# The third pass of key and value products in the wide attentions, split over two halves of the array and the unused rows of another pass

## The chip, the cores and the metric

One core of a Trainium2 chip runs the whole program in one launch. The metric is device time in microseconds (us) of that execution; the time of the kernel before is the median of three runs. TensorE multiplies on a 128x128 array, ScalarE, VectorE and GpSimd (POOL in the profile) do elementwise work, and SyncE (SP) issues DMAs. Results of TensorE go to PSUM, whose eight banks hold 512 fp32 columns each.

## The reference

A stack of four pairs of layers, each a cross-attention and a feed-forward part, all added to a residual x of 128 batches x 64 rows x 128 channels. Three of the four cross-attentions are wide (layers 0, 1 and 3 of the reference): 8, 8 and 16 heads of 64 channels, over a context of 64 rows x 96 channels per batch.

```python
x = x + jnp.tanh(g_xattn[0]) * _L0_xattn_ref(_layernorm(x, axis=-1), ctx_768, mask_BxS2_bk0, ...)
...
# in a wide attention
q = (x @ W_q).reshape(b, n, HEADS, DIM_HEAD)
k = (context @ W_k).reshape(b, j, HEADS, DIM_HEAD)
v = (context @ W_v).reshape(b, j, HEADS, DIM_HEAD)
sim = jnp.einsum('bihd,bjhd->bhij', q, k) * scale
attn = jax.nn.softmax(jnp.where(mask, sim, max_neg), axis=-1)
out = jnp.einsum('bhij,bjhd->bihd', attn, v).reshape(b, n, INNER)
return out @ W_o + b_o
```

Layer 3 has one more key and value per head (null_kv), a layernorm with a gain before, and another behind. All is fp32. The change touches only how k and v are computed from the context.

## The kernel before

**Stages.** `program` runs eight stages one after another. Stages 0, 2 and 6 call `wide_attention` for layers 0, 1 and 3; `null` is true for layer 3. In the trace they lie at about 0 to 325 us, 965 to 1300 us and 2325 to 2985 us.

**Groups, units, tiles.** x has 64 tiles of 128 rows (two batches of 64), in 16 groups of TG = 4. A unit (`Unit`) is one group with eight heads: layers 0 and 1 have 16 units, layer 3 has 32 (two passes over a group, u = 0 and u = 1). Every engine walks the same loop: iterations `it`, two units `u`, four tiles `t`, one `step` each, so 64, 64 and 128 steps, 256 in all. The first and the last iteration are written out, the ones between are a loop on the chip.

**Three products for one.** An fp32 product is made of three fp32r products: each operand is split into a high part and the rest, high x high, high x low and low x high are summed in PSUM (`product3`, whose lines L384, L385 and L386 name the three). `ch`/`cl` are the parts of the transposed context of a unit (96 channels on partitions 0 to 95, 512 columns), `kh`/`kl`, `qh`/`ql`, `wvh`/`wvl` those of the weights. The values need a layout of their own, `vh`/`vl`, which POOL makes from `ch`/`cl` (`spread`, L576 and L577). In layer 3 partition 96 of `vh` and `wvh` carries the null value.

**One step of TensorE**, in the order of its queue: transpose the probabilities of tile n (L778), project the output of tile n-1 (L722), `attend` (L712, 64x64 tiles of the array), `scores` of tile n+2 (L700, 64x64 tiles), in some steps `turn` (L669: transpose the normed rows of a later group into hT), `value_job` of tile n+1 (six products of 256 columns), `key_job` (three products of 512 columns with 96 rows) and `query_job` (three products of 512 columns with 128 rows) for a later unit. `turn` comes where t = 1: in every unit of layers 0 and 1 but the last two, and in layer 3 with u = 0 only. `target_of` says which unit the keys are for: a unit's first two key blocks are made at t = 2 and 3 two units ahead, the others at t = 0 and 1 one unit ahead. The last iteration has keys in its first two steps only.

**Banks and waits.** Keys go to bank 1, queries to bank 0, values to bank 4, but to bank 0 for t = 1; the transposes (L778 and L669) use bank 4 as well. ScalarE empties them in this order in each step: transposed probabilities (L912), queries of the step before (L833), attention output (L919, L921), then hT (L842, where there is a turn), values (L837), the high part of hT (L846), keys (L828), exponentials of tile n+2 (L850). In layer 3 the high part of hT comes last, after the queries. TensorE's query at t = 1 waits for `v_done` (the value copy, same bank), its attend for `pt_out` (L912), its scores at t = 2 for the last query copy (L833).

**Context.** SP loads the raw context of a unit (L528), waiting for `low`; POOL splits it at t = 0 two units ahead (L561 high, L563 low, after its wait `k_done`). In layer 0 SP issues the loads of everything later (`boot.sync_third`, L193 and L195) between the first iteration's waits and the loop:

```python
            n = units // 2
            body(0, False)
            if boot:
                boot.sync_third(sp)
            if n > 3:
                with sp.Fori(1, n - 2) as it:
                    body(it, False)
```

Of the kernel before, what the change touches and what calls it, by code (L numbers as in the profile page):

```python
# [5 lines left out]
FP = mybir.dt.float32  # L6
# [422 lines left out]
def wide_attention(c, d, layer, boot=None):  # L429
# [34 lines left out]
    hh, hl = [r([GT]) for _ in range(nhq)], [r([GT]) for _ in range(nhq)]  # L464
    (kh, kl), (qh, ql), (wvh, wvl) = ((r([WN]), r([WN])) for _ in range(3))
    if masked:
        mask = c.mask
        nm = [w([TG, SW]), w([TG, SW])]
    if null:
# [19 lines left out]
    o_ready, ot_out, acc_ready, added, nm_ready = (sem(n) for n in ("o", "ot_out", "acc", "added", "nm"))  # L489
    acc_out, edges = sem("acc_out"), sem("edges")  # L490
    fin_bn, fin_mv, fin_eps, fin_rstd, fin_y, fin_yg = (
        sem(n) for n in ("fbn", "fmv", "feps", "frstd", "fy", "fyg"))
# [31 lines left out]
    with nc.Block() as block:  # L524
        @block.sync
        def _(sp):
# [8 lines left out]
            if boot:  # L535
                boot.sync_second(sp)

            def body(it, last):
# [126 lines left out]
        def _(te):  # L665
# [16 lines left out]
            def value_job(un, t, out):  # L682

                if t == 0:
                    te.wait_ge(spread_ready, un.k * 2 + 2)
                for e in range(2):
                    at = (un.p * 2 + e) * NJ * DH
                    lhs = [v[un.u][0:VR, t, e:e + 2, :].rearrange("c b k -> c (b k)") for v in (vh, vl)]
                    last = product3(c, out[:, e * NJ * DH:(e + 1) * NJ * DH], lhs, [v[0:VR, at:at + NJ * DH] for v in (wvh, wvl)])
                last.then_inc(v_full, 1)  # L690
# [77 lines left out]
            def step(it, u, t, last):  # L768
# [21 lines left out]
                if t < 2 or not end:  # L790
# [6 lines left out]
                    scores(n + 2, *two_on(un, t))  # L797
                if turns(u, t, last):
                    turn(un.g + 1 if null else un.k + 2)
                if not (end and t == TG - 1):  # L800
                    if t == 1 and had_target(it, u, t, last):
                        te.wait_ge(q_done, n + 6)
# [22 lines left out]
        def _(act):  # L825
# [48 lines left out]
            if null:  # L874
                for i in range(2):
                    last_row = slice(DC, DC + 1)
                    ones = bc(c.w["ones"][last_row, :], 1, TG * 3 * S // P)
                    A.activation(vh[i][last_row, :, :, :].rearrange("c t b k -> c (t b k)").rearrange("c (n k) -> c n k", k=P), ones, ACT.Copy,
                                 scale=-1.0)
                    A.activation(vl[i][last_row, :, :, :].rearrange("c t b k -> c (t b k)").rearrange("c (n k) -> c n k", k=P), ones, ACT.Copy,  # L880
                                 scale=0.0)
# [24 lines left out]
            def body(it, last):  # L906
                for u in range(2):
                    for t in range(TG):
# [1689 lines left out]
def program(nc, d, layers=range(8)):  # L2598

    ctx = ExitStack()  # L2600
    with ctx:
# [15 lines left out]
        for layer in layers:  # L2617

            parts = {0: 8 * GT + 12 * P * 2 + 24 * D, 2: 8 * GT + 12 * P * 2 + 24 * D, 5: 4 * GT + 4 * W2N, 6: 6 * GT + 12 * P * 2 + 48 * D}
            c.open_work({0: 15 * 1024, 2: 15 * 1024, 6: 14 * 1024, 5: 12 * 1024}.get(layer, 26 * 1024) - TG * P, parts.get(layer, 0))  # L2620
            if layer in (0, 2, 6):
# [98 lines left out]
```

## Time and profile before

| | |
|---|---|
| median of 3 runs | 3075.03 us (3073.38 to 3079.5) |
| profiled execution | 3082.58 us, span of its instructions 3080.6 us |
| granted TensorE clock, mean | 0.977 |
| TensorE busy | 2901.3 us (94%) |
| VectorE busy | 2225.0 us (72%) |
| ScalarE busy | 1579.8 us (51%) |
| POOL busy | 1182.4 us (38%) |
| DMA | 211.98 MB |

The profile is one execution. Matmuls are pipelined: the duration that a row gives runs to the end of the last column, so rows overlap and starts tell more than durations. A product's start is that of its slot in the array; where its weights could not be loaded ahead, the load is inside its slot, and shows as a later start of the product behind it. A time in a row of the timeline is the start from the beginning of the span.

### The profile page before, as it was taken

The numbers are of one execution on the slowest core, as the hardware profiler recorded it, in microseconds if no ns is written. First come the engines' busy times: TensorE is split into PE (matmuls) and PEld (weight loads), VectorE is DVE, ScalarE is ACT, GpSimd is POOL, SyncE is SP. The second block draws the span as 40 slices with busy tenths as digits, with TensorE's granted clock in tenths as the row PEclk, the third lists the DMA queues.
The fourth block names the chain that finished last, engine by engine and source line by source line (L and its number), as shares of the span: only waits on it lengthen the run. The fifth ranks groups of instructions, "written<-read, shape, count | busy, mean of one in ns | idle before, by whom it ended". The sixth has DMA issues, their size and how long they took to land. (4 is left out here: it accounts for less than half of the span.)

```text
span 3080.6 us, 89544 instructions
## 1 busy us (share of the span) xinstructions
PE 2901.3 (94%) x34642; PEld 2264.9 (74%) x34642; DVE 2225.0 (72%) x5778; ACT 1579.8 (51%) x2906; POOL 1182.4 (38%) x1274
## 2 busy tenths in 40 slices
PE   7999799999998999859997999999998999999978
PEld 6888545555546888746666888888886888888864
DVE  6777666666655666568887777788766788878766
ACT  6777311211113777537774333333336777777756
POOL 6677200000003777564450000000004677777753
PEclk9999899999999999979998999999998999999989
DMA  5000166666661000011111333323330000000001
GB/s 157 20 10 8 62 187 178 182 181 179 184 169 35 12 10 10 2 52 27 25 26 57 111 105 104 105 97 96 106 112 16 12 10 9 9 10 10 10 1 55
DMA packets 110872, 211.98 MB, mean 69 GB/s; under 512 B 18738, under 2 KB 30450, under 8 KB 110195
## 3 DMA queue, kind: packets, MB, share of 16 engines
q1 hardware_dynamic: 110194, 208.98, 22.8%
q8 instruction: 89, 1.46, 0.2%
q10 hardware_dynamic: 512, 0.92, 0.1%
q14 instruction: 77, 0.62, 0.1%
HBM read 198.29 MB, written 5.77 MB: 66 GB/s over the span
## 5 line engine op out<-in xcount | busy, mean ns | idle before, releaser
L384 PE MATMUL ps<-parts 128*128 128x512 f32 (+3 forms) x1568 | 623.3, 398 | 34.1 <-DVE parts L1002 18.2
L385 PE MATMUL ps<-parts 128*128 128x512 f32 (+3 forms) x1568 | 565.1, 360 | 0.0
L386 PE MATMUL ps<-parts 128*128 128x512 f32 (+3 forms) x1568 | 563.7, 359 | 0.0
L318 POOL TENSOR_TENSOR rstd<-mv,eps 128x4 f32<-128x4 f32 x106 | 21.2, 200 | 998.4 <-DVE mv L301 998.2
L1941 ACT ACTIVATE work<-ps 128x512 f32<-128x512 f32 x272 | 162.5, 598 | 441.9 <-PE ps L386 441.7
L384 PEld LDWEIGHTS ps<-parts 128*128 128x128 f32 (+2 forms) x1568 | 299.4, 191 | 106.3 <-ACT work L837 26.4
L582 POOL TENSOR_TENSOR work<-work 128x512 f32<-128x512 f32 x256 | 266.9, 1043 | 278.1 <-DVE work L972 278.1
L386 PEld LDWEIGHTS ps<-parts 128*128 128x128 f32 (+2 forms) x1568 | 298.8, 191 | 46.0
L385 PEld LDWEIGHTS ps<-parts 128*128 128x128 f32 (+2 forms) x1568 | 301.2, 192 | 20.6
L1906 PEld LDWEIGHTS ps<-early,work 128*128 128x128 f32 x2176 | 281.5, 191 | 18.8 <-DVE pause L1995 0.3
L1906 PE MATMUL ps<-early,work 128*128 128x128 f32 x2176 | 288.0, 275 | 0.1
L1991 DVE TENSOR_TENSOR work<-work,ps 128x512 f32<-128x512 f32 x272 | 185.7, 683 | 122.0 <-PE ps L1906 107.5
L970 DVE TENSOR_REDUCE work<-work 128x8 f32<-128x512 f32 (+1 forms) x256 | 174.0, 680 | 127.1 <-ACT work L850 125.5
L2276 PE MATMUL ps<-work,early 128*128 128x512 f32 x512 | 248.1, 607 | 1.3 <-DVE work L2518 1.3
L837 ACT ACTIVATE work<-ps 128x512 f32<-128x512 f32 x256 | 153.1, 598 | 149.1 <-PE ps L386 146.1
L958 DVE SCALAR_TENSOR_TENSOR ps<-ps,work 128x520 f32<-128x520 f32 (+1 forms) x192 | 135.2, 704 | 130.6 <-PE ps L700 130.0
L962 DVE TENSOR_REDUCE work<-ps 128x8 f32<-128x512 f32 (+1 forms) x256 | 178.0, 695 | 53.8 <-PE ps L700 47.1
L712 PE MATMUL ps<-work 64*64 64x64 f32 x8192 | 179.3, 224 | 11.6 <-ACT work L912 9.5
L2518 DVE TENSOR_TENSOR work<-work 128x1024 f32<-128x1024 f32 x128 | 154.7, 1219 | 47.5 <-DMA work<-gate_rows 45.5
L2001 DVE TENSOR_TENSOR work<-work 128x512 f32<-128x512 f32 x256 | 177.2, 692 | 12.7 <-DVE work L1991 0.2
L964 DVE TENSOR_TENSOR work<-ps,work 128x512 f32<-128x512 f32 (+1 forms) x256 | 178.0, 695 | 8.8
L712 PEld LDWEIGHTS ps<-work 64*64 64x64 f32 x8192 | 145.4, 134 | 44.5 <-issue 16.9
(296 smaller groups left out, 6072.6 us busy)
## 6 DMA issues: line engine op xcount, KB each, us to landing
work<-gate_rows SPq DMA_DIRECT2D x128, 512.0 KB, 5.7
work<-expert_rows SPq DMA_DIRECT2D x512, 128.0 KB, 2.9
work<-gate_rows SPq DMA_DIRECT2D x128, 256.0 KB, 7.0
work<-in_ctxT SPq DMA_DIRECT2D x72, 192.0 KB, 2.4
out<-x SPq DMA_DIRECT2D x16, 256.0 KB, 2.3
work<-work SPq DMA_DIRECT2D x224, 16.0 KB
work<-work SPq DMA_DIRECT2D x16, 128.0 KB, 2.3
early<-in_l0f_w SPq DMA_DIRECT2D x1, 1536.0 KB
```

What stands on the lines that cost most here:

```text
L384: T.matmul(out, lh, rh, start=True, stop=False)
L385: T.matmul(out, lh, rl, start=False, stop=False)
L386: return T.matmul(out, ll, rh, start=False, stop=True)
L582: G.tensor_tensor(pn[t % 2], pr[t % 2][:, :, 0:S], bc(rec[t % 2], 2, S), ALU.mult).then_inc(p_ready, 1)
L712: last = T.matmul(ps_o[e * DH:e * DH + DH, b, j, :], vp[t % 2][rows, e, j, :], ptT[rows, j, b * S:b * S + S], start=True, stop=True)
L962: V.tensor_reduce(mx[t % 2], ps_s, AX.X, ALU.max).then_inc(max_ready, 1)
L964: V.tensor_tensor(sc[t % 2].rearrange("p (j s) k -> p s j k", s=2), ps_s.rearrange("p (s j) k -> p s j k", s=2), bc(tops, 3, SW), ALU.subt ...
L970: V.tensor_reduce(den[t % 2], pr[t % 2], AX.X, ALU.add).then_inc(sum_ready, 1)
L1906: last = T.matmul(acc[u][:, t * D:(t + 1) * D], aT[b][:, t * P:(t + 1) * P], c.w["l2f_d"][:, j, :], start=(j == 0 and t == 0), stop=(j == ...
L1991: out = V.tensor_tensor(aT[b], sg[b], ps_u[b], ALU.mult)
L2001: V.tensor_tensor(aT[b], aT[b], wb[j % WR], ALU.mult).then_inc(a_ready, 1)
L2276: T.matmul(ps_q[u], c.w["l0f_w"][:, at:at + P], hw[p % NHW][:, e, :], start=(p == 0 and e == 0), stop=(p == NP - 1 and e == 1))
```

## The change

The low x high product of keys and values is cut in two. Of the 96 rows of the high x low pass, 32 are put beside the 96 rows of the low x high pass (partitions 96 to 127, which were idle), and the other 64 become products of their own on half of the array: for the keys on partitions 64 to 127 (`key_third`), for the values on partitions 0 to 63 (`value_third`), issued one behind the other, with different banks. Both come right after the scores; then the rest of the values, the turn, the rest of the keys, the query. ScalarE copies the values before hT. Which of the rows lie where:

- keys, half product: weights `kl` 64 to 127, data `ch` 64 to 127; rows 96 to 127 hold copies of rows 0 to 31;
- keys, 128-row product: `kh` and `cl`, whose rows 96 to 127 hold copies of rows 32 to 63 of `kl` and `ch`;
- values, half product: `vh` and `wvl`, rows 0 to 63; 128-row product: `vl` and `wvb`, whose rows 96 to 127 hold rows 64 to 95 of the context's high part and of `wvl`. `wvb` is `wvh` itself, and a buffer of its own in layer 3.

The copies are made by DMAs from SBUF to SBUF that SP issues. Layer 3's prologue loses two activations that set the null row of `vl` to zero (L880), and the null row's low part moves into row 97 of `wvh`.

```diff
+            def rows_for_keys(un):
+                sp.wait_ge(high, un.k + 1)
+                sp.dma_start(plain(ch[un.u][DC:P, :]), plain(ch[un.u][0:P - DC, :])).then_inc(key_rows[un.u], 16)
+                sp.dma_start(plain(cl[un.u][DC:P, :]), plain(ch[un.u][P - DC:S, :])).then_inc(key_rows[un.u], 16)
+            def rows_for_values(un):
+                src = plain(ch[un.u][S:DC, :]).rearrange("c (t b k) -> c t b k", b=2, k=S)
+                sp.dma_start(plain(vl[un.u][DC:P, :, 0:2, :]), src).then_inc(value_rows[un.u], 16)
+                sp.dma_start(plain(vl[un.u][DC:P, :, 2, :]), src[:, :, 0, :]).then_inc(value_rows[un.u], 16)
+            rows_for_keys(first)
+            rows_for_values(first)
+            sp.wait_ge(w_low, passes)
+            sp.dma_start(plain(kl[DC:P, :]), plain(kl[0:P - DC, :])).then_inc(weight_rows, 16)
+            sp.dma_start(plain(kh[DC:P, :]), plain(kl[P - DC:S, :])).then_inc(weight_rows, 16)
+            rows_for_keys(second)
+            rows_for_values(second)
+            sp.wait_ge(w_low, 3 * passes)
+            sp.dma_start(plain(wvb[DC:P, :]), plain(wvl[S:DC, :])).then_inc(weight_rows, 16)
...
             def body(it, last):
                 for u in range(2):
                     un = Unit(it, u, passes)
+                    rows_for_keys(un.next().next())
                     if not (u == 1 and isinstance(it, int) and it == units // 2 - 2):
                         sp.wait_ge(low, un.k + 3)
                         load(cs, cs_in, un.next().next().next())
+                    sp.wait_ge(v_full, un.k * 4 + 4)
+                    rows_for_values(un.next().next())
...
                 if raw is cs:
                     pool.wait_ge(cs_in, (un.k - 1) * 16)
+                    pool.wait_ge(value_rows[un.u], un.it * 32)
...
+            def key_third(un, j, bank):
+                T.matmul(jobs[bank], kl[S:P, at:at + P], ch[un.u][S:P, :], start=True, stop=False)
+            def key_rest(un, j, bank):
+                T.matmul(jobs[bank], kh[0:DC, at:at + P], ch[un.u][0:DC, :], start=False, stop=False)
+                T.matmul(jobs[bank], kh[:, at:at + P], cl[un.u], start=False, stop=True).then_inc(k_full, 1)
+            def value_third(un, t, out):
+                for e in range(2):
+                    T.matmul(out[:, e * NJ * DH:(e + 1) * NJ * DH], vh[un.u][0:S, t, e:e + 2, :].rearrange("c b k -> c (b k)"),
+                             wvl[0:S, at:at + NJ * DH], start=e == 0, stop=False, skip_group_check=True)
+            def value_rest(un, t, out):
+                for e in range(2):
+                    T.matmul(dst, high_rows[0:VA, :], wvh[0:VA, cols], start=False, stop=False, skip_group_check=True)
+                    last = T.matmul(dst, low_rows, wvb[:, cols], start=False, stop=e == 1, skip_group_check=True)
...
-                if turns(u, t, last):
-                    turn(un.g + 1 if null else un.k + 2)
-                if not (end and t == TG - 1):
-                    value_job(*one_on(un, t), value_bank(t))
-                if has_target(u, t, last):
-                    key_job(target, j, 1)
+                if opening:
+                    te.wait_ge(weight_rows, WEIGHT_ROWS)
+                if keys:
+                    if t == 2 or opening:
+                        te.wait_ge(key_rows[target.u], target.it * 32 + 32)
+                    key_third(target, j, 1)
+                if values:
+                    if t == TG - 1 or opening:
+                        te.wait_ge(value_rows[value_unit.u], value_unit.it * 32 + 32)
+                    value_third(value_unit, value_tile, value_bank(t))
+                    value_rest(value_unit, value_tile, value_bank(t))
+                if turns(u, t, last):
+                    turn(un.g + 1 if null else un.k + 2)
+                if keys:
+                    key_rest(target, j, 1)
...
+                        if not (end and t == TG - 1):
+                            take_values(n + 1, t + 1, value_bank(t))
                         if turns(u, t, last):
                             take_hT(un.g + 1 if null else un.k + 2)
-                        if not (end and t == TG - 1):
-                            take_values(n + 1, t + 1, value_bank(t))
```

## Rows read from the trace of the kernel before

**Rows 1.** Windows: each engine's busy us, clock, DMA; layer 3's loop.

```profile
2370.00:2970.00 600.00, 594.57 (x10775) 519.09 (x10774) 475.00 (x1169) 452.32 (x800) 419.48 (x428) 1.00 0.03 10
```

**Rows 2.** Timeline of TensorE, a plain step of layer 1: start, duration, line.

```profile
1120.30 0.38 PE L384 MATMUL ps<-parts 96*128 96x256 f32 x1
1120.53 0.28 PE L385 MATMUL ps<-parts 96*128 96x256 f32 x1
...
1121.12 0.40 PE L384 MATMUL ps<-parts 96*128 96x512 f32 x1
...
1121.81 0.40 PE L384 MATMUL ps<-parts 128*128 128x512 f32 x1
```

**Rows 3.** Timeline of TensorE where the form of the tile changes, other stages.

```profile
514.61 1.16 PE L2296 MATMUL ps<-work 64*128 64x128 f32 x8
515.70 1.12 PE L2276 MATMUL ps<-work,early 128*128 128x512 f32 x2
...
3031.73 1.14 PE L1692 MATMUL ps<-work,l3f_v 32*128 32x512 f32 x8
3032.80 1.12 PE L1684 MATMUL ps<-work,l3f_u 128*128 128x512 f32 x2
```

**Rows 4.** Timeline of ScalarE, a step with a turn in layer 1.

```profile
1071.53 0.60 ACT L842 ACTIVATE work<-ps 128x512 f32<-128x512 f32 x1 [0.50 <-PE ps L669]
1072.16 0.60 ACT L837 ACTIVATE work<-ps 128x512 f32<-128x512 f32 x1
1072.65 0.62 ACT L846 ACTIVATE parts<-work 128x512 fp32r<-128x512 f32 x1
...
1073.66 0.63 ACT L850 ACTIVATE work<-work 128x512 f32<-128x512 f32 x1
1074.25 0.60 ACT L912 ACTIVATE work<-ps 128x512 f32<-128x512 f32 x1
1074.74 0.59 ACT L833 ACTIVATE work<-ps 128x512 f32<-128x512 f32 x1
```

**Rows 5.** Timeline of TensorE in the same step and the next.

```profile
1070.76 0.66 PE L669 MATMUL ps<-ident,hn 128*128 128x128 f32 x4
...
1072.81 0.50 PE L384 MATMUL ps<-parts 128*128 128x512 f32 x1
...
1073.61 0.60 PE L778 MATMUL ps<-ident,work 128*128 128x128 f32 x4
1074.05 1.06 PE L722 MATMUL ps<-early,work 128*128 128x128 f32 x8
...
1075.68 0.69 PE L700 MATMUL ps<-work 64*64 64x64 f32 x32
```

**Rows 6.** Timelines of ScalarE and TensorE, layer 3, u = 1, t = 1.

```profile
2539.95 0.60 ACT L837 ACTIVATE work<-ps 128x512 f32<-128x512 f32 x1 [0.66 <-PE ps L386]
2540.61 0.50 PE L384 MATMUL ps<-parts 128*128 128x512 f32 x1
```

**Rows 7.** Timeline of SP in layer 0: first load of `sync_third`, next context load.

```profile
57.65 0.43 SPq L193 DMA_DIRECT2D l_wo<-in_l_wo  x1
...
88.99 0.35 SPq L528 DMA_DIRECT2D work<-in_ctxT  x1
```

**Rows 8.** Timeline of ScalarE in layer 0: copy of unit 1's last values.

```profile
65.41 0.60 ACT L837 ACTIVATE work<-ps 128x512 f32<-128x512 f32 x1 [0.75 <-PE ps L386]
```

**Rows 9.** Timeline of TensorE in layer 0, unit 2: t = 0 and t = 2.

```profile
77.24 0.58 PE L384 MATMUL ps<-parts 96*128 96x256 f32 x1
...
81.25 1.06 PE L778 MATMUL ps<-ident,work 128*128 128x128 f32 x4
...
90.33 0.39 PE L384 MATMUL ps<-parts 96*128 96x256 f32 x1
```

**Rows 10.** DMA issues of the page: count, KB each, us from issue to landing.

```profile
work<-in_ctxT SPq DMA_DIRECT2D x72, 192.0 KB, 2.4
```

**Rows 11.** One line's instructions (L880): duration ns min/median/max, first and last start.

```profile
L880 ACT ACTIVATE parts<-ones x2: 822/822/823, 2329.8 to 2331.7; 1x768 fp32r<-1x768 f32 x2
```

More of the change, by code:

```diff
@@ L465, in wide_attention @@
     (kh, kl), (qh, ql), (wvh, wvl) = ((r([WN]), r([WN])) for _ in range(3))
+    wvb = r([WN]) if null else wvh
+    plain = lambda ap: ap.bitcast(FP)
     if masked:
@@ L490, in wide_attention @@
     acc_out, edges = sem("acc_out"), sem("edges")
+    weight_rows = sem("weight_rows")
+    key_rows, value_rows = [sem(f"key_rows{u}") for u in range(2)], [sem(f"value_rows{u}") for u in range(2)]
+    WEIGHT_ROWS = 16 * (5 if null else 3)
     fin_bn, fin_mv, fin_eps, fin_rstd, fin_y, fin_yg = (
@@ L536, in _ @@
                 boot.sync_second(sp)
+            def rows_for_keys(un):
[15 more added lines that the diff above has]
+            sp.dma_start(plain(wvb[DC:P, :]), plain(wvl[S:DC, :])).then_inc(weight_rows, 16)
+            if null:
+                sp.dma_start(plain(wvb[0:DC, :]), plain(wvh[0:DC, :])).then_inc(weight_rows, 16)
+                sp.dma_start(plain(wvh[DC + 1:DC + 2, :]), plain(wvl[DC:DC + 1, :])).then_inc(weight_rows, 16)
             def body(it, last):
@@ L682, in value_job @@
             def value_job(un, t, out):
-                if t == 0:
-                    te.wait_ge(spread_ready, un.k * 2 + 2)
+                te.wait_ge(spread_ready, un.k * 2 + 2)
                 for e in range(2):
                     at = (un.p * 2 + e) * NJ * DH
-                    lhs = [v[un.u][0:VR, t, e:e + 2, :].rearrange("c b k -> c (b k)") for v in (vh, vl)]
-                    last = product3(c, out[:, e * NJ * DH:(e + 1) * NJ * DH], lhs, [v[0:VR, at:at + NJ * DH] for v in (wvh, wvl)])
+                    cols = slice(at, at + NJ * DH)
+                    dst = out[:, e * NJ * DH:(e + 1) * NJ * DH]
+                    high_rows, low_rows = (v[un.u][:, t, e:e + 2, :].rearrange("c b k -> c (b k)") for v in (vh, vl))
+                    T.matmul(dst, high_rows[0:VR, :], wvh[0:VR, cols], start=True, stop=False)
+                    T.matmul(dst, high_rows[0:VR, :], wvl[0:VR, cols], start=False, stop=False)
+                    last = T.matmul(dst, low_rows[0:DC, :], wvh[0:DC, cols], start=False, stop=True)
@@ new lines, in value_job @@
+                last.then_inc(v_full, 1)
+            def key_third(un, j, bank):
+                at = un.p * NJ * P + j * P
+                T.matmul(jobs[bank], kl[S:P, at:at + P], ch[un.u][S:P, :], start=True, stop=False)
+            def key_rest(un, j, bank):
+                at = un.p * NJ * P + j * P
+                T.matmul(jobs[bank], kh[0:DC, at:at + P], ch[un.u][0:DC, :], start=False, stop=False)
+                T.matmul(jobs[bank], kh[:, at:at + P], cl[un.u], start=False, stop=True).then_inc(k_full, 1)
@@ L797, in step @@
                     scores(n + 2, *two_on(un, t))
-                if turns(u, t, last):
-                    turn(un.g + 1 if null else un.k + 2)
-                if not (end and t == TG - 1):
-                    if t == 1 and had_target(it, u, t, last):
-                        te.wait_ge(q_done, n + 6)
-                    value_job(*one_on(un, t), value_bank(t))
-                if has_target(u, t, last):
+                values, keys = not (end and t == TG - 1), has_target(u, t, last)
+                opening = isinstance(it, int) and it == 0 and u == 0 and t == 0
+                if opening:
+                    te.wait_ge(weight_rows, WEIGHT_ROWS)
+                if keys:
                     target, j = target_of(un, t)
@@ L811, in step @@
                         te.wait_ge(low, target.k + 1)
-                    key_job(target, j, 1)
+                    if t == 2 or opening:
+                        te.wait_ge(key_rows[target.u], target.it * 32 + 32)
+                    key_third(target, j, 1)
+                if values:
+                    if t == 1 and had_target(it, u, t, last):
+                        te.wait_ge(q_done, n + 6)
+                    value_unit, value_tile = one_on(un, t)
+                    if t == TG - 1:
+                        te.wait_ge(spread_ready, value_unit.k * 2 + 2)
+                    if t == TG - 1 or opening:
[6 more added lines that the diff above has]
+                    key_rest(target, j, 1)
                     if t == 1:
@@ L2617, in program @@
         for layer in layers:
-            parts = {0: 8 * GT + 12 * P * 2 + 24 * D, 2: 8 * GT + 12 * P * 2 + 24 * D, 5: 4 * GT + 4 * W2N, 6: 6 * GT + 12 * P * 2 + 48 * D}
-            c.open_work({0: 15 * 1024, 2: 15 * 1024, 6: 14 * 1024, 5: 12 * 1024}.get(layer, 26 * 1024) - TG * P, parts.get(layer, 0))
+            parts = {0: 8 * GT + 12 * P * 2 + 24 * D, 2: 8 * GT + 12 * P * 2 + 24 * D, 5: 4 * GT + 4 * W2N, 6: 6 * GT + 12 * P * 2 + 56 * D}
+            c.open_work({0: 15 * 1024, 2: 15 * 1024, 6: 14 * 1024 - 256, 5: 12 * 1024}.get(layer, 26 * 1024) - TG * P, parts.get(layer, 0))
             if layer in (0, 2, 6):
```

14 lines of the change are left out of this document (9 added, 5 removed).

## The prediction

> **What bounds the kernel now.** I read first the busy time of each engine over the steady part of the last wide attention, which is the longest. TensorE is busy 594.6 of 600 us there, at the full 2.4 GHz clock (granted 1.00), ScalarE 452 [rows 1]. So a step (one 128-row tile, eight heads) lasts as long as TensorE's own order of work, and what TensorE's queue gains or loses per step is gained or lost 256 times, unless a wait stands behind it. Second, TensorE's timeline of one plain step [rows 2]: from the first value product to the first query product it is 1121.81 - 1120.30 = 1.51 us. The reader should see two spacings in it. A 256-column product follows the one before after 0.12 us ((1121.12 - 1120.53)/5), a 512-column one after 0.23 us ((1121.81 - 1121.12)/3); but the first value product, which comes right after the 64x64 scores, holds its successor up by 0.23 instead of 0.12. Third, other stages, for what happens where the form of the tile changes [rows 3]. Fourth, ScalarE's and TensorE's timelines around the turn of hT [rows 4, 5] and in the second tile of a group without one [rows 6], since ScalarE's order is edited. Last, SP's queue in layer 0 [rows 7 to 9], since new waits go into it.
>
> **What the packed third is worth.** Removed from TensorE's stream: one 512-column key product (0.23) that now runs beside two 256-column value products (2 x 0.12). Do halves run side by side? In the low-rank stage four row groups with two passes each, all 128 columns wide into four banks, take 3032.80 - 3031.73 = 1.07 us for eight 512-column passes [rows 3], when even eight fp32r products at 0.23 would need 1.84 one after another. So yes.
>
> Added: one more change of tile form. Before, a step goes 128-wide to 64x64 (attend, scores) to 128-wide; now 64x64 to 64x128 to 128x128. The price: eight 64-row passes between two 128-row stages take 515.70 - 514.61 = 1.09 us [rows 3]. Such a 128-column pass is 0.11 in the unbroken stream of transposes ((1074.05 - 1073.61)/4 [rows 5]), 0.89 for eight: 0.20 more, and 0.11 of it is the weight load that is not hidden behind a product (as 0.23 against 0.12 in [rows 2]), 0.09 a drain. The Trainium skill's page "TensorEngine Tiling (Array Packing)", Key Properties, says that changing the tiling mode drains TensorE. The trace agrees, with these 0.09 us for each change; the page has no price and says nothing of the weight load behind it.
>
> New stretch, from the same start T: load 0.11, first value third 0.12, second 0.12 (the key third ends in the same time, 0.11 + 0.23), drain 0.09 gives the form 128x128 at T+0.43; load 0.11, four value products 0.47, two key products 0.46: the query begins at T+1.475. Gain 0.035 us per plain step instead of the 0.23 that the packing seems to offer. Bounds for the change 64x64 to 64x128, which no row shows: nothing (gain 0.235), or as much as every other change (0.035). I take the latter, because a change of rows alone and of both dimensions costs the same in [rows 3].
>
> A step with values but no keys (5 at each layer's end) only pays: 2 x 0.12 + 0.20 - 2 x 0.12 = 0.20.
>
> **ScalarE.** The value copy starts when the last value product ends. That product now starts at T+0.89 instead of T+0.70 (0.23 + 4 x 0.12), so v_done is 0.19 later although the query is due earlier. The product is 0.28 long [rows 2] and the copy starts some 0.04 after its end (an estimate by the 0.06 between copy and query in [rows 6]): T+1.21. In the second tile (t = 1) the values lie in bank 0, which the query needs.
> Without a turn (layer 3, second unit): the query begins 0.06 after the end of the copy already, 2540.61 against 2539.95 + 0.60 [rows 6], and this moves by +0.19. Cost +0.19 for 15 steps.
> With a turn (T' = 1070.76, start of the transposes): before, the query starts at T'+2.05, held by the copy; then the next step's transposes at T'+2.85, its scores at T'+4.92 [rows 5]. Now the turn stands between values and keys, and the query is free: transposes at T'+0.89+0.12+0.44+0.46+0.70 = T'+2.61. But ScalarE's chain starts at T'+1.21 instead of T'+0.77 (1071.53 [rows 4]): value copy 1.21, hT 1.70 (spacing 0.49 as 1072.16 to 1072.65), its high part 2.33 (it needs the finished hT, 0.60, and a little), key copy and exponentials in the spacing 1.01 of 1072.65 to 1073.66: 3.34, then the copy of the transposed probabilities 0.49 to 0.59 later (the latter in 1073.66 to 1074.25, where it waited for TensorE), I take 0.53, 3.87, the query copy 0.49 on, 4.36, done 4.95. Scores begin 0.35 after that end now (1075.68 against 1074.74 + 0.59 [rows 4, 5]): T'+5.30. So this step loses 0.38 where it should win 0.035. It comes 14 times in each of layers 0 and 1. In layer 3 the high part is made after the queries, outside this chain: between 0 and 0.38, I take 0.10, 15 times.
>
> Sums: layers 0 and 1, 28 units x (0.38 - 3 x 0.035) = +7.7. Layer 3, 15 pairs of units x (0.10 + 0.19 - 5 x 0.035, the first step of a group gaining nothing since it waits for the copy of acc) = +1.7. Layer ends 15 x 0.20 = +3.0.
>
> **SP's queue in layer 0.** The new rows are filled by DMAs that SP issues, two for keys and two for values a unit: 32 rows of 2 KB each, landing some 2.4 us after issue like the context load [rows 10]. In steady state the key rows are issued when POOL has the high part in t = 0 and are read in t = 2, two steps on; value rows have five steps. Hidden. Not so once: after the first pair of units SP issues the loads of all later layers. That took from 57.65 to 88.99, 31.3 us [rows 7]. Before, it began when POOL had split unit 3. Now SP first waits for all values of unit 1 (v_full), which ScalarE takes at 65.41 [rows 8], then issues two more: start 66.4, end 97.7, and only behind it come the key rows of unit 4, landing about 97.7 + 0.9 + 2.4 = 101. TensorE wants them with the key third at 90.33 [rows 9], shifted by about 0.4: a pause of 10.3 us. Queued behind that wait is everything on TensorE, so also ScalarE, VectorE and POOL. After an idle stretch it restarts at 1.2 GHz: 81.25 - 77.24 = 4.01 us from value to transposes [rows 9] against 1.51 + 0.70 in [rows 2], 1.8 more; with the following step 2.5. Sum +12.8. Bounds: 0 if the rows land in time, 16 if the later loads also run slower beside them.
> In layer 0's prologue the weight rows and first rows queue behind the loads of x and are due with the first step; I take nothing, bounds 0 and one landing, 2.4 [rows 10]. In layer 3's prologue two activations of 0.82 us go, ahead of the first key copies [rows 11]: between 0 and -1.64, I take -0.95, since hT's copy behind them also waits for transposes.
>
> Sum: 7.7 + 1.7 + 3.0 + 12.8 - 0.95 = +24.3 us. The profiled execution took 3082.6 (span 3080.6); against it 3106.9, against the median of the runs, 3075.0, it is 3099.3.
>
> **Rivals.**
> (a) The change 64x64 to 64x128 is free, because rows stay at 64. Then 238 steps with both thirds and 15 without keys win 0.20 each: 3099 - 51 = 3048, faster. For it: no row shows this pair. Against: every pair that is shown pays. It decides from about half the price: with under 0.10 saved per step the kernel is still not faster. 14%.
> (b) No pause in layer 0 (SP is through earlier, or rows overtake the loads): 3099 - 13 = 3086, still slower. For it: the last nine loads are limited by issue, not by data. 15%.
> (c) ScalarE keeps up in the turn steps, whose wait for the value copy (0.26) then vanishes: 28 x (0.38 + 0.26) = 18 less, 3081. With (b) 3068. For it: ScalarE has 25% free; against: the chain above. 10%, a third of it with (b).
> (d) The halves do not run side by side: 238 x 0.23 more, 3154. For it: no fp32r product with 64 rows is shown. The Trainium skill's page "TensorE: Matmul & The Clock Gate", Measured speedup vs the span model, gives 3.07 for four row tiles instead of 4; by that the pair would take 0.31 instead of 0.24, an estimate of 238 x 0.07 = 16 us more. 6%.
> My forecast (all prices as worked out) has 55%; its own range is 3088 to 3112.
>
> **How the numbers follow.** A measurement tells 0.2% (6 us) from no change. Faster: (a) and (b with c), 18%, and a little for (c) turning out better: 20%. Same: what is left of (c) and of mixed cases, 8%. Slower 72%. For 8 in 10 the range leaves out most of (a) and (d) and takes in (b), (c): 3070 to 3115.
>
> **What the profile after would show.** TensorE's plain step: L700, then a 512-column product and two 256-column ones within 0.01 and 0.23 us, the first 128x128 product 0.43 after the block's start; step length 4.68 instead of 4.72. In t = 1 with a turn the next scores some 0.38 later, with ScalarE without a gap from value copy to query copy. One pause of TensorE near 91 us, released by a DMA. Wrong if plain steps are 4.5 us (a), 4.9 (d), if no pause is there (b), or if turn steps shrink (c).

## The result, and the profile after

The changed kernel takes 3111.53 us (median of 4 runs, 3109.38 to 3113.28) against 3074.35 before (4 runs, 3073.38 to 3079.5): 1.0113 times as long, 95% interval 1.0101 to 1.0126. The forecast was 3099.3, slower. Its profiled execution took 3113.28 us with a span of 3111.3, 30.7 more than the profiled execution before; the medians differ by 37.2. Against its own median the profile before lies 8.2 us high and that after 1.8, so 6.5 us of the difference cannot be placed in the two traces.

The length of a step below is the distance between the first transposes of successive steps (L778 before, L845 after). Over the 64, 64 and 128 steps of the three wide attentions the distance from the first to the last grew from 318.2 to 341.0 us (layer 0), 306.5 to 311.7 (layer 1) and 628.5 to 631.8 (layer 3): 31.3 in all, as much as the two spans differ by. Within the kinds of step it looks like this (medians, us; where a row has values for odd and even units, units are counted from 0, so even is u = 0):

| step | before | after |
|---|---|---|
| layer 1, t = 0 / t = 3 | 4.716 / 4.718 | 4.713 / 4.714 |
| layer 1, t = 1 (turn) | 5.367 | 5.197 |
| layer 1, t = 2 (odd / even units) | 4.773 / 4.900 | 5.223 / 5.462 |
| layer 3, u = 0: t = 1 (turn), t = 2 | 5.759, 5.027 | 5.559, 5.343 |
| layer 3, u = 1: t = 1 | 4.991 | 5.187 |
| layer 1, the five last steps with values and no keys | 4.27, 4.30, 4.30, 3.36, 4.41 | 4.46, 4.49, 4.50, 3.56, 4.53 |

First the plain step. TensorE's timeline of the kernel after, layer 1 (start, duration, line), to be read against [rows 2]:

```profile
1105.81 0.50 PE L732 MATMUL ps<-parts 64*128 64x512 f32 x1
1105.81 0.50 PE L744 MATMUL ps<-parts 64*128 64x256 f32 x2
1106.24 0.38 PE L755 MATMUL ps<-parts 96*128 96x256 f32 x1
1106.46 0.28 PE L756 MATMUL ps<-parts 128*128 128x256 f32 x1
1106.59 0.28 PE L755 MATMUL ps<-parts 96*128 96x256 f32 x1
1106.71 0.28 PE L756 MATMUL ps<-parts 128*128 128x256 f32 x1
1106.82 0.40 PE L737 MATMUL ps<-parts 96*128 96x512 f32 x1
1107.07 0.40 PE L738 MATMUL ps<-parts 128*128 128x512 f32 x1
1107.30 0.40 PE L384 MATMUL ps<-parts 128*128 128x512 f32 x1
```

The key half product (L732) and the first value half product (L744) start together, and the first product on the whole array (L755, 96 of its rows, form 128x128) follows 0.43 us later. Then see the four starts from 1106.24 on: the first successor comes after 0.22, the others after 0.12 or 0.13. That 0.22 is the second change of form, paid as at the first product before. Three whole products have become three halves that share their time, and two changes of form are there where one was: from the block's start to the query it is 1.49 us, against 1.51.

Second, the turn. ScalarE's timeline of the kernel after, a step with a turn in layer 1, against [rows 4]; the block of half products starts at T' = 1115.24:

```profile
1116.46 0.60 ACT L918 ACTIVATE work<-ps 128x512 f32<-128x512 f32 x1 [0.95 <-PE ps L756]
1116.95 0.59 ACT L923 ACTIVATE work<-ps 128x512 f32<-128x512 f32 x1
1117.58 0.63 ACT L927 ACTIVATE parts<-work 128x512 fp32r<-128x512 f32 x1
1118.11 0.58 ACT L909 ACTIVATE work<-ps 128x512 f32<-128x512 f32 x1
1118.59 0.62 ACT L931 ACTIVATE work<-work 128x512 f32<-128x512 f32 x1
1119.11 0.59 ACT L991 ACTIVATE work<-ps 128x512 f32<-128x512 f32 x1
1119.59 0.60 ACT L914 ACTIVATE work<-ps 128x512 f32<-128x512 f32 x1
```

Seven activations without a gap. Counted from T', values, hT, its high part, exponentials, transposed probabilities and queries start at 1.22, 1.71, 2.34, 3.35, 3.87 and 4.35; the forecast had 1.21, 1.70, 2.33, 3.34, 3.87 and 4.36. TensorE in the same step, against [rows 5]:

```profile
1115.24 0.50 PE L732 MATMUL ps<-parts 64*128 64x512 f32 x1
...
1117.17 0.44 PE L384 MATMUL ps<-parts 128*128 128x512 f32 x1
...
1117.92 0.60 PE L845 MATMUL ps<-ident,work 128*128 128x128 f32 x4
...
1119.84 0.69 PE L779 MATMUL ps<-work 64*64 64x64 f32 x32 [0.43 <-ACT work L991]
1120.33 0.68 PE L767 MATMUL ps<-work 64*64 64x64 f32 x32
```

TensorE is done with its turn step earlier, and then its attend (L779) stands 0.43 us for the copy of the transposed probabilities (L991), the sixth link of ScalarE's chain. So t = 1 shrinks and t = 2 grows by more. This is an odd unit, where the scores (L767) follow the attend by 0.49. In the even units of the same layer the attend stands 0.46 for the same copy and the scores follow it by 0.69; they begin 0.35 after the end of the query copy (L914), as they do in the even units of the kernel before. Counted from T', scores begin at 5.09 in odd units and 5.32 in even ones, against 4.79 and 4.92 before. In layer 3 with u = 1, where there is no turn, the query waits for the value copy, both 0.19 later, against [rows 6]:

```profile
2567.22 0.60 ACT L918 ACTIVATE work<-ps 128x512 f32<-128x512 f32 x1 [0.86 <-PE ps L756]
...
2567.86 0.50 PE L384 MATMUL ps<-parts 128*128 128x512 f32 x1 [0.21 <-ACT work L918]
```

Third, layer 0. TensorE's timeline and then SP's of the kernel after, against [rows 7 to 9]:

```profile
86.94 0.69 PE L767 MATMUL ps<-work 64*64 64x64 f32 x32
104.73 0.79 PE L732 MATMUL ps<-parts 64*128 64x512 f32 x1 [17.10 <-DMA parts<-parts]
...
108.61 1.05 PE L845 MATMUL ps<-ident,work 128*128 128x128 f32 x4
```

```profile
68.34 0.59 SPq L193 DMA_DIRECT2D l_wo<-in_l_wo  x1
...
98.65 0.43 SPq L195 DMA_DIRECT2D tri<-in_tri  x1
99.31 0.56 SPq L546 DMA_DIRECT2D parts<-parts  x1
99.92 0.58 SPq L547 DMA_DIRECT2D parts<-parts  x1
```

One pause of 17.1 us, ended by a DMA from SBUF to SBUF. SP spends 68.34 to 99.31 on the loads of later layers, and only behind them it issues the key rows (L546, L547) of unit 4. Behind the pause TensorE runs slowly, at a granted clock of 0.50 from 104 to 108 us: from block to transposes it is 3.88 us, against 2.17 us in the next step (112.03 to 114.20). The waits of TensorE over the whole program (total us, count, longest) put the two that grew side by side (for the first, the kernel before has 9.5 us in 14 waits), and the windows of layer 3, against [rows 1], show that there the array stays the bound:

```profile
PE ps L779 <- ACT work L991: 24.1, 52, 1.5
PE ps L732 <- DMA parts<-parts: 18.4, 2, 17.1
```

```profile
2400.00:3000.00 600.00, 587.46 (x10684) 501.01 (x10682) 471.05 (x1163) 436.05 (x794) 416.35 (x425) 1.00 0.08 21
```

### The profile page after: what moved, and what is told of

It is laid out like the page before. It is cut to its first block and busy times, and to the rows that moved or that the text cites. A ratio compares the mean times of both kernels' runs of the same rounds, so it can differ in the third digit from the quotient of the medians.

```text
span 3111.3 us, 90063 instructions
## 1 busy us (share of the span) xinstructions
PE 2897.9 (93%) x34642; PEld 2240.0 (72%) x34642; DVE 2224.8 (72%) x5778; ACT 1552.7 (50%) x2904; POOL 1181.2 (38%) x1274
## 5 line engine op out<-in xcount | busy, mean ns | idle before, releaser
L384 PE MATMUL ps<-parts 128*128 128x512 f32 (+1 forms) x818 | 356.7, 436 | 37.6 <-DVE parts L1081 17.8
L386 PE MATMUL ps<-parts 128*128 128x512 f32 (+1 forms) x818 | 325.7, 398 | 0.0
L385 PE MATMUL ps<-parts 128*128 128x512 f32 (+1 forms) x818 | 325.6, 398 | 0.0
L1985 PEld LDWEIGHTS ps<-early,work 128*128 128x128 f32 x2176 | 281.8, 192 | 18.9 <-DVE pause L2074 0.3
L384 PEld LDWEIGHTS ps<-parts 128*128 128x128 f32 (+1 forms) x818 | 157.3, 192 | 86.9 <-ACT work L918 21.6
L779 PE MATMUL ps<-work 64*64 64x64 f32 x8192 | 178.6, 224 | 24.6 <-ACT work L991 24.1
L779 PEld LDWEIGHTS ps<-work 64*64 64x64 f32 x8192 | 145.4, 135 | 58.4 <-issue 34.6
L386 PEld LDWEIGHTS ps<-parts 128*128 128x128 f32 (+1 forms) x818 | 156.0, 191 | 37.4
L610 POOL TENSOR_TENSOR parts<-parts,zero 96x512 fp32r<-96x512 f32 x128 | 166.5, 1300 | 27.6 <-ACT parts L948 27.6
```

Source lines behind the costliest of these rows:

```text
L384: T.matmul(out, lh, rh, start=True, stop=False)
L385: T.matmul(out, lh, rl, start=False, stop=False)
L386: return T.matmul(out, ll, rh, start=False, stop=True)
L779: last = T.matmul(ps_o[e * DH:e * DH + DH, b, j, :], vp[t % 2][rows, e, j, :], ptT[rows, j, b * S:b * S + S], start=True, stop=True)
L1985: last = T.matmul(acc[u][:, t * D:(t + 1) * D], aT[b][:, t * P:(t + 1) * P], c.w["l2f_d"][:, j, :], start=(j == 0 and t == 0), stop=(j == ...
```

## The experiments

All ratios are against the kernel before, run on the same chip (medians 3076.5 to 3078.6 there).

**One: the later loads in parts** (`e1_loads_in_parts`). `sync_third` is cut into four parts, one in each of the units 1 to 4, so that the copies queue behind seven or so loads instead of all.

```diff
                         load(cs, cs_in, un.next().next().next())
+                    if boot and isinstance(it, int) and it * 2 + u in (1, 2, 3, 4):
+                        boot.sync_part(sp, it * 2 + u - 1)
                     sp.wait_ge(v_full, un.k * 4 + 4)
```

> The changed kernel, but in layer 0 SP issues the loads of the later layers in four parts, one in each of units 1 to 4, behind that unit's key rows and ahead of its wait for the values. My theory (the pause of 17.1 us near 87 us is key rows queued behind 31 us of loads): pause and the slow-clock restart behind it go, 19 to 20 us less, about 3091. Rival 1, the copies from SBUF to SBUF are themselves late while anything loads: a pause of several us stays, 5 us less at most. Rival 2, the time is lost elsewhere and the pause was hidden: no change, 3111.

3093.04 us (3089.99 to 3094.71), ratio 1.0043 [1.0026, 1.0060]. Layer 0 is 19.7 us shorter than after the change, 18.9 of it in the step that held the pause; layers 1 and 3 do not move. TensorE of this kernel at the same place:

```profile
87.17 0.69 PE L771 MATMUL ps<-work 64*64 64x64 f32 x32
87.80 0.50 PE L736 MATMUL ps<-parts 64*128 64x512 f32 x1
```

The half product (L736 here) follows the scores at once. The pause is the place of the copies in SP's queue and nothing else.

**Two: hT's high part a step later** (`e2_high_part_later`). ScalarE makes it after the query copy of the turn step, POOL's split moves behind `spread`.

```diff
+                        if turns(u, t - 1, last) and not null:
+                            rows_high(un.k + 2, u)
                         act.wait_ge(o_ready, n + 1)
...
-                        if turns(u, t, last) and not null:
-                            rows_high(un.k + 2, u)
```

> The changed kernel, but in layers 0 and 1 ScalarE makes the high part of hT one step later, behind the query copy of t = 2, and POOL spreads the values' low part before it splits hT. My theory (ScalarE's chain from value copy to query copy holds up attend and scores of t = 2): step t = 2 goes from 5.22 to about 4.77 us, 28 times, 12 to 13 us less, about 3099. Rival, another wait holds t = 2 (POOL's split or the keys): t = 2 stays above 5.1 us and the time moves by less than 3 us, or gets worse because hq_low comes late.

3096.12 us, ratio 1.0059 [1.0042, 1.0076]. In layer 1 step t = 2 goes from 5.223 and 5.462 (odd and even units) to 4.711 and 4.896; over the 14 units that is 7 to 8 us for each of layers 0 and 1. ScalarE's timeline of this kernel:

```profile
1104.37 0.64 ACT L931 ACTIVATE work<-work 128x512 f32<-128x512 f32 x1
1105.02 0.60 ACT L991 ACTIVATE work<-ps 128x512 f32<-128x512 f32 x1
1105.51 0.59 ACT L914 ACTIVATE work<-ps 128x512 f32<-128x512 f32 x1
1105.99 0.63 ACT L927 ACTIVATE parts<-work 128x512 fp32r<-128x512 f32 x1
```

The block of this step starts at 1101.70, so the copy of the probabilities (L991) begins at T' + 3.32 instead of 3.87, and the high part (L927) fills the place where ScalarE otherwise waits. The stall was the order of ScalarE's chain, not its load.

**Three: whole products in the new order** (`e3_whole_thirds`). Everything of the change stays, copies and waits too, but the third pass goes over its 96 rows in one piece, and the 128-row products over 96.

```diff
-                T.matmul(jobs[bank], kl[S:P, at:at + P], ch[un.u][S:P, :], start=True, stop=False)
+                T.matmul(jobs[bank], kl[0:DC, at:at + P], ch[un.u][0:DC, :], start=True, stop=False)
...
-                    last = T.matmul(dst, low_rows, wvb[:, cols], start=False, stop=e == 1, skip_group_check=True)
+                    last = T.matmul(dst, low_rows[0:DC, :], wvb[0:DC, cols], start=False, stop=e == 1, skip_group_check=True)
```

> The changed kernel in its new order and with all its copies, but the third pass is one whole product of 96 rows (97 for null values) for the keys and for each half of the values, so there is one change of tile form less and nothing beside it. My theory (the half products win 0.235 us per step, the extra drain and the weight load take 0.20 back and the products with 128 rows 0.03): plain step 4.716 us, and the layers' last steps 0.2 shorter each, in all 3108 (3104 to 3113). Rival, the drain is not the price and the new order or the copies cost the time: plain step 4.65 or less would be seen, 3095 or less. Rival 2, the halves do win something net: 3120 or more.

3115.8 us (3113.11 to 3116.55), ratio 1.0121 [1.0104, 1.0138], above the range that I had given and not clearly apart from the changed kernel's 1.0113. The plain step is 4.7355, against 4.716 before and 4.713 after. So the half products win 0.022 us net per plain step, but the new order with whole products loses 0.02 against the old one. The timelines show where: the 256-column products, which now stand behind a 512-column one, follow one another after 0.120 us instead of 0.116 to 0.119 (means of layer 1, t = 0), while the 512-column ones keep their distances. Why is not shown.

**Four: both half products on the same half** (`e4_same_half`). The key half product uses rows 0 to 63 instead of 64 to 127, so its sum has other rows in it.

```diff
-                T.matmul(jobs[bank], kl[S:P, at:at + P], ch[un.u][S:P, :], start=True, stop=False)
+                T.matmul(jobs[bank], kl[0:S, at:at + P], ch[un.u][0:S, :], start=True, stop=False)
```

> The changed kernel, but the keys' half product takes rows 0 to 63 instead of 64 to 127, the same half of the array as the values' (so other rows are summed; the sizes are the same). My theory (the halves do run side by side): the key third and the two value thirds then follow one another, the first 128-row product comes 0.66 instead of 0.43 us after the block's start, plain step 4.95, and about 56 to 60 us more, near 3169. Rival (they never ran side by side, or the array shares one stream of moving data): no change, 3111.

3164.75 us, ratio 1.0279 [1.0259, 1.0300]; the plain step 4.911. TensorE's timeline of this kernel:

```profile
1122.28 0.49 PE L732 MATMUL ps<-parts 64*128 64x512 f32 x1
1122.62 0.39 PE L744 MATMUL ps<-parts 64*128 64x256 f32 x2
1122.94 0.39 PE L755 MATMUL ps<-parts 96*128 96x256 f32 x1
```

On one half they take turns, 0.66 us to the first whole-array product instead of 0.43. So on two halves they run at the same time in full; that is worth 0.23 us in the block and 0.20 in the plain step.

**Five: one more change of form** (`e8_one_more_change`). The order is rest of the values, half products, rest of the keys, so that the step has one more pair of 128-row and 64-row stages.

```diff
-                    value_third(value_unit, value_tile, value_bank(t))
                     value_rest(value_unit, value_tile, value_bank(t))
+                if keys:
+                    key_third(target, j, 1)
+                if values:
+                    value_third(value_unit, value_tile, value_bank(t))
```

> The changed kernel with the same products, but the half products stand between the rest of the values and the rest of the keys: the form of the tile goes 64x64, 128x128, 64x128, 128x128, one change more in each step. My theory (a change costs a drain of 0.09 us and a weight load of 0.11): plain step 4.91 us, 0.20 x 241 = 48 us more than the changed kernel and a few more where the value copy is late, ratio near 1.028. Rival, the extra change is cheap and something else eats the gain: plain step 4.75 or less.

3144.86 us, ratio 1.0218 [1.0197, 1.0238]; the plain step is 4.89, 0.18 more than after the change. TensorE's timeline of this kernel:

```profile
1112.44 0.28 PE L757 MATMUL ps<-parts 128*128 128x256 f32 x1
1112.65 0.50 PE L732 MATMUL ps<-parts 64*128 64x512 f32 x1
1112.66 0.50 PE L744 MATMUL ps<-parts 64*128 64x256 f32 x2
1113.08 0.50 PE L737 MATMUL ps<-parts 96*128 96x512 f32 x1
1113.41 0.40 PE L738 MATMUL ps<-parts 128*128 128x512 f32 x1
```

The half products start 0.21 behind a 256-column product instead of 0.12, and the product after the one at 1113.08 comes 0.33 later instead of 0.23. A drain of 0.09 and an uncovered weight load of 0.10 for the additional change, as forecast from other stages. The total grew by 33 us and not by 48. Turn steps grew by only 0.08 to 0.09 and the u = 1, t = 1 step of layer 3 not at all: there the wait for ScalarE covered it. And layer 0's first step, 8.75 us after the change, is 6.19 here, a difference that does not come from this edit (see what the traces differ in, below).

**Six: without the copied rows** (`e9_copied_rows_out`). The rows 96 to 127 are left out of the 128-row products, so the sum lacks 32 rows.

```diff
-                T.matmul(jobs[bank], kh[:, at:at + P], cl[un.u], start=False, stop=True).then_inc(k_full, 1)
+                T.matmul(jobs[bank], kh[0:DC, at:at + P], cl[un.u][0:DC, :], start=False, stop=True).then_inc(k_full, 1)
```

> The changed kernel, but the second product of each rest takes 96 rows instead of 128 (the 32 copied rows of high times low are left out of the sum); everything else, the copies too, stays. The plain step won 0.003 us instead of the 0.035 that I worked out, because the products after the block follow one another 0.003 to 0.012 later than before. Theory A, the switch between 96 and 128 rows costs it: spacings of 0.232 again, plain step 4.68 us, 6 to 8 us less than the changed kernel. Theory B, it is the moment at which these products run, beside what the other engines do, and not their rows: plain step stays 4.71, no change in all.

3111.55 us, ratio 1.0112 [1.0091, 1.0133]. In layer 1 the plain step is 4.688, so 0.025 shorter, which is what theory A asks; the total is that of the changed kernel, and two runs cannot tell 6 us from nothing. The traces show less than 6: layers 1 and 3 are 1.1 us shorter each, since in layer 3 the plain steps won 0.01 to 0.04 and both steps with t = 1 lost 0.02. TensorE's timeline of this kernel:

```profile
1105.13 0.40 PE L737 MATMUL ps<-parts 96*128 96x512 f32 x1
1105.37 0.40 PE L738 MATMUL ps<-parts 96*128 96x512 f32 x1
1105.60 0.40 PE L384 MATMUL ps<-parts 128*128 128x512 f32 x1
```

The last five 512-column products of a plain step of layer 1 (two of the keys, three of the query) take 1.187 us in the kernel after, spaced 0.243, 0.237, 0.240, 0.235 and 0.231; before they take 1.156, here 1.163, and in experiment four, with the same 128 rows, 1.149 at t = 0 and 1.168 at t = 3. So the number of rows alone does not set them.

**Seven: both stalls mended** (`e5_halves_mended`). Experiments one and two together, the high part later in layer 3 too, and whole products where a step has no keys.

```diff
+                    if keys:
+                        value_third(value_unit, value_tile, value_bank(t))
+                        value_rest(value_unit, value_tile, value_bank(t))
+                    else:
+                        value_job(value_unit, value_tile, value_bank(t))
```

> The changed kernel with everything mended that the runs so far showed: the loads of layer 0 in four parts, the high part of hT one step later in all three layers, and whole products in the few steps without keys. My theory (the parts add up): against the changed kernel 20 + 15 + 3 for the layers' ends + some 4 in layer 3 = 42 us less, ratio to the kernel before 0.997 to 1.000. Rival, the half products still win something once the waits are gone: 0.992 or less.

3068.41 us (3062.99 to 3070.47), ratio 0.9969 [0.9958, 0.9981]: faster than before, by little.

**Eight and nine: the new order without any half product.** `e6_before_new_order` is the kernel before with only the order of values and turn changed, on TensorE and on ScalarE; `e7_before_order_and_high` has the high part a step later besides.

```diff
-                if turns(u, t, last):
-                    turn(un.g + 1 if null else un.k + 2)
                 if not (end and t == TG - 1):
...
                     value_job(*one_on(un, t), value_bank(t))
+                if turns(u, t, last):
+                    turn(un.g + 1 if null else un.k + 2)
```

> The kernel before, no halves and no copies, only with the new order: values before the turn on TensorE, value copy before hT on ScalarE. My theory: the turn step no longer waits for the value copy (t = 1 from 5.37 to 5.16 us in layers 0 and 1, from 5.76 to 5.55 in layer 3), while ScalarE's chain, 0.19 us earlier than with the halves, makes t = 2 about 0.2 later, so nearly nothing: ratio 0.998 to 1.002. Rival, the new order alone costs what the changed kernel lost in these steps: 1.003 or more.

> The same, and the high part of hT made one step later (all three layers), POOL's spread ahead of the split. My theory: t = 1 as in the kernel with the order alone, t = 2 near 4.75 us in all layers: 28 x 0.3 + 15 x 0.4 = 14 us less than before, ratio 0.9955, the best of all without any half product. Rival, the late split of hT holds up the query of t = 2 (hq_low): ratio 1.000 or more.

The order alone: 3081.34 us, 1.0016 [1.0006, 1.0025]. In layer 1 its turn step falls from 5.367 to 5.167, and t = 2 rises from 4.773 and 4.900 to 5.092 and 5.292. With the high part later: 3064.29 us (3062.99 to 3065.44), 0.9954 [0.9938, 0.9971]; 5.163, and again 4.773 and 4.90, in layer 1, 5.541 and 4.898 in layer 3. ScalarE's timeline of this kernel, in a turn step whose block starts at 1082.46:

```profile
1083.47 0.60 ACT L837 ACTIVATE work<-ps 128x512 f32<-128x512 f32 x1 [0.74 <-PE ps L386]
1083.96 0.59 ACT L842 ACTIVATE work<-ps 128x512 f32<-128x512 f32 x1
...
1085.75 0.60 ACT L912 ACTIVATE work<-ps 128x512 f32<-128x512 f32 x1
1086.24 0.59 ACT L833 ACTIVATE work<-ps 128x512 f32<-128x512 f32 x1
1086.72 0.63 ACT L846 ACTIVATE parts<-work 128x512 fp32r<-128x512 f32 x1
```

The copy of the probabilities (L912) begins at T' + 3.29, before TensorE's attend wants it (the attend starts at T' + 4.08, without a wait). The high part a step later in the old order was not run, so the two edits are known together and the order alone, but not the high part alone.

**Ten: half products except in the second tile** (`e10_halves_but_second`). The kernel of experiment seven, but at t = 1 whole products for keys and values.

```diff
-                    key_third(target, j, 1)
+                    if t != 1:
+                        key_third(target, j, 1)
```

> The mended kernel with the halves, but in the second tile of each unit (t = 1), where the query waits for the value copy, values and keys are whole products in the order of before. My theory (in t = 1 the halves only delay the value copy by 0.19 us; elsewhere they win next to nothing): layer 3's second unit from 5.19 back to 4.99 us, 15 times, 3 us less than the mended kernel, ratio to before 0.995 to 0.997, the same as the kernel without halves (0.9954). Rival, halves win where they can: below 0.993.

3064.5 us (3060.6 to 3067.46), ratio 0.9957 [0.9943, 0.9972]; the step with u = 1, t = 1 is back at 4.987. This equals the second kernel of eight and nine, which has no half product and no copied row: even with every new wait taken away, the packed third pass wins nothing that the runs can tell (in the traces layer 1 is 0.6 us shorter than in that kernel, layer 3 as long). The gain on the kernel before is that of the order together with the later high part.

## Why the forecast was right, and where its terms were off

**The direction and its cause: right.** The packing looks worth 0.235 us a step and is worth almost none, because the second change of form gives back 0.20. The drain and the uncovered load are in the trace after, and experiment five buys them once more for 0.18. Rival (a), a free change, is excluded: plain steps would be 4.5 us. Rival (d) is excluded by experiment four. Rival (c) is excluded by the chain of seven activations, whose six forecast starts are hit within 0.01; rival (b) by the pause. One sign was badly chosen: the prediction would have taken shrinking turn steps for rival (c), and they did shrink, by 0.17, because their own wait for the value copy is gone; the loss stands in the step behind, and only the two together tell.

**The plain step: mechanism right, size off.** Won 0.003 instead of 0.035. The block up to the first whole-array product took the forecast 0.43; the loss is in the five 512-column products behind, whose spacing I took over unchanged from the kernel before. They take 1.187 us instead of 1.156. The sum used 0.035 won three times in each of the 28 units of layers 0 and 1 and five times in each of 15 pairs of units in layer 3. In layers 0 and 1 two such steps stand beside the turn's pair of steps, 1.8 us more than forecast; in layer 3 the five steps together are 0.02 longer where 0.175 was to be won, 2.9 us more.

**The turn: right.** The steps t = 1 and t = 2 together lose 0.34 us in layer 1 (-0.17 and +0.51 from the second unit on; the first unit's turn step is 0.9 shorter), forecast 0.38 - 0.035 = 0.345. The forecast used an even unit (scores at T' + 4.92), where the query copy does release the scores: they moved to 5.32, forecast 5.30. In odd units, which it did not look at, what ends last is the attend's wait for the copy of the probabilities, and the scores moved from 4.79 to 5.09. Layer 1 in all is 5.2 longer, forecast 3.85 and 1.0 for its end. In layer 3 the turn's pair of steps loses 0.10 to 0.12 and u = 1, t = 1 loses 0.196, forecast 0.10 and 0.19. With the plain steps that makes 0.33 for each pair of units, forecast 0.115. The layer is 3.4 longer, forecast 1.7 + 1.0; that this is near is luck, since the first pair of units, 1.5 us shorter, and the layer's end make up for the plain steps.

**Steps with values alone: the price right, the count wrong.** Forecast 15 x 0.20 = 3.0. In layer 1 the five steps lose 0.19, 0.19, 0.20, 0.20 and 0.12. In layer 0 only the first of them loses 0.19 and the others nothing; in layer 3 one loses 0.40, a later one wins 0.29, and the five together lose 0.10. In all it is 1.2. What holds the last steps of layers 0 and 3 was not looked into.

**The pause: the mis-sized term.** Forecast 10.3 + 2.5 = 12.8; the step grew by 19.4. Three parts of 10.3 were off. TensorE stood ready at about 87.6 instead of 90.7. Part of that is the ninth step of layer 0: in the trace of the kernel before it takes 8.98 us, with TensorE idle for 0.78 and 1.85 us and a granted clock of 0.57 from 76 to 84 us, and 4.73 after. The kernel of experiment nine, without any copy, has 4.78 there, so this is not the work of the change. SP's loads began at 68.34 instead of 66.4 and took 31.0. And of the two copies that TensorE waits for, right behind 30 loads, the first landed 2.4 us after its issue at 99.31, as forecast, but the second, issued at 99.92, 4.8 after it, at 104.69. The restart took 2.3 us, forecast 2.5. Experiment one gets back 19.7.

**What the two traces differ in besides.** Layer 0's first step is 3.3 longer. The opening waits, bounded by 2.4 and taken at nothing, are 1.3 of it at most (one wait of 1.30 us for copied rows). The granted clock is 0.57 from 28 to 36 us, where the kernel before has 1.00. Over all twelve traces this goes with TensorE's start and not with the change: where the first transposes of layer 0 start at 25.7 to 26.1 us the first step takes 8.1 to 9.3 and that clock is 0.50 to 0.79, and where they start at 27.1 to 28.0 it takes 5.4 to 6.2 at 1.00. The order alone, without any new wait, is of the first kind (8.08, clock 0.58), and experiment three, with all of them, of the second (5.70, clock 1.00). Between the last step of layer 0 and the first of layer 1 it is 2.7 us more, 640.7 against 637.9. The other kernels have 638.6 to 641.0 there, so that cannot be put down to the change. Between those of layers 1 and 3, with layer 3's prologue, it is 1.3 less, forecast -0.95; but the order alone, which keeps both activations, has 1058.4 there, against 1058.2 after and 1059.5 before, so the term is not shown. Sum of the forecast 24.3, of the profiles 30.7, of the medians 37.2. In the first gap of 6.4 the pause alone is 6.6, and the other errors, in both directions, cancel nearly: that they do is luck; the second is the two profiled executions' distance from their medians and stays unplaced.

## What to carry to other kernels

Before splitting a product to fill idle rows of the array, count the changes of tile form in the loop, at the price that the kernel's own trace shows for one (here 0.2 us, nearly as much as a 512-column product takes), and look whether the new form can be put next to one that is there already. Copies that a loop needs soon must not share a queue with a batch of loads: find the longest burst on that queue and the consumer's start in the trace. And when an edit reorders a chain on another engine, try the order by itself: here the order alone won nothing (1.0016), and the only gain (0.9954) came when, besides, the one activation that nobody was waiting for was moved behind the two that TensorE needed. Last, before a difference between two traces is called an effect, see whether other kernels with the same code at that place differ as much.

## What the runs showed of the hardware

- A change of tile form costs 0.09 us of drain and 0.10 to 0.11 of weight load that nothing hides (both read from distances between starts), here between 64x64, 64x128 and 128x128 tiles, whether rows, columns or both change.
- fp32r products of 64 rows on the two halves of the array run side by side in full: 0.43 us instead of 0.66 for one of 512 and two of 256 columns.
- Spacing of 512-column fp32r products is not a constant: five of them take 1.156 us before and 1.187 in the packed block (0.243 at most for one). Leaving rows 96 to 127 idle took 0.025 off layer 1's plain step, but with the same 128 rows, behind half products that took turns, the five took 1.149 to 1.168. The cause is open.
- The granted clock of TensorE was 0.50 in the first microseconds behind the pause of 17.1 us, and steps there took 3.88 us for what took 2.17 in the next step. From 28 to 36 us it was 0.50 to 0.79 in eight traces and 1.00 in four, with and without the change in both groups.
- SBUF-to-SBUF copies of 32 rows landed 2.0 us after issue (median of 198); right behind a burst of 30 loads one landed 2.4 and the next 4.8 us after issue.
